# Attention's last two batches interleaved with the first expert slots, x rows scattered one iteration earlier, slot rows in grouped loads

## The reference

```python
q, k, v = heads(x, Wq, bq), heads(x, Wk, bk), heads(x, Wv, bv)      # 16 heads of 8
qp = relu(einsum('bhsd,hdf->bhsf', q, rw)) + 1e-6                   # 64 features a head
kp = relu(einsum('bhsd,hdf->bhsf', k, rw)) + 1e-6
kv = einsum('bhsf,bhsd->bhfd', kp, v)
out = einsum('bhsf,bhfd->bhsd', qp, kv) / (einsum('bhsf,bhf->bhs', qp, kp.sum(axis=2))[..., None] + 1e-6)
attention = out.reshape(b, s, 128) @ Wo + bo

probs = softmax(x @ wr + br)                                        # 8 experts
top_p, top_i = top_k(probs, 2)
gate, top1 = top_p[:, 0] / (top_p[:, 0] + top_p[:, 1]), top_i[:, 0]
for e in range(8):                                                  # w1: 128 x 512, w2: 512 x 128
    hout = gelu(x @ w1[e] + b1[e], approximate=False) @ w2[e] + b2[e]
    out = out + where(top1 == e, hout * gate, 0)
```

## Time and profile before

| | us |
|---|---|
| median of three executions | 260.04 |
| lowest, highest | 259.35, 261.4 |
| the profiled execution, its own time | 258.03 |
| its span in the profile | 256.3 |
| granted clock of PE over the span | 0.96 |
| busy: PE, PEld | 211.7 (83%), 170.2 (66%) |
| busy: DVE, ACT, POOL | 121.3 (47%), 125.4 (49%), 114.6 (45%) |
| the chain that ended last: PE, DVE, DMA | 68%, 8%, 7% |

### The profile page before, as it was taken

One profiled execution on the slowest core, in us unless ns is written; L12 is line 12 of the kernel. 1 busy time (PEld: TensorE's weight loads), 2 busy tenths in 40 slices (PEclk: granted clock), 3 DMA queues, 4 the chain that ended last, 5 costly groups with the idle time before them and its releaser, 6 DMA issues.

```text
span 256.3 us, 6785 instructions
## 1 busy us (share of the span) xinstructions
PE 211.7 (83%) x2370; PEld 170.2 (66%) x2370; DVE 121.3 (47%) x386; ACT 125.4 (49%) x291; POOL 114.6 (45%) x170
## 2 busy tenths in 40 slices
PE   0499897566899999999999689288799999999920
PEld 0365664344577676667776578187799999999920
DVE  4737532577777776777676424113233333333210
ACT  2184496333565555566655544124355555555500
POOL 3984460113667444444443425205545544445540
PEclk9999999799999999999999979769999999999995
DMA  5539999700341111111111321275888878887100
GB/s 127 157 120 345 335 278 284 207 3 12 86 146 55 64 44 42 44 44 44 43 44 64 79 72 34 63 212 145 224 259 222 234 206 236 244 237 193 57 18 0
DMA packets 27749, 34.12 MB, mean 133 GB/s; under 512 B 5523, under 2 KB 19127, under 8 KB 27718
## 3 DMA queue, kind: packets, MB, share of 16 engines
q1 hardware_dynamic: 24372, 27.24, 38.9%
q0 software_dynamic: 2944, 6.37, 7.2%
q10 hardware_dynamic: 402, 0.09, 0.2%
HBM read 22.11 MB, written 14.12 MB: 141 GB/s over the span
## 4 chain that ended last, share of the span: by engine, by line
PE 68%; DVE 8%; DMA 7%; issue 4%; ACT 4%; SPq 3%; POOL 3%; ACTq 0%; POOLq 0%; DVEq 0%
PE feat L584 12%; PE feat L480 7%; PE o_bank L598 6%; PE kv_bank L491 6%; PE kt_bank L598 6%; PE feat L469 5%; PE o_bank L515 5%; PE o_bank L524 3%; PE w_bank L533 3%; PE feat L440 2%; DVE k_feat L860 2%; DMA slot_rows<-sorted_r 2%; DMA w_slot<-w1x 2%; PE feat L441 2%; PE kt_bank L500 1%
## 5 line engine op out<-in xcount | busy, mean ns | idle before, releaser
L737 ACT ACTIVATE q_all<-feat,w_slot 128x128 f32<-128x128 f32 x156 | 44.5, 368 | 48.4 <-PE feat L584 48.4
L417 POOL DMA_INDIRECT out<-k_all,slot_rows x39 | 38.3, 983 | 47.1 <-DVE k_all L934 29.0
L584 PE MATMUL feat<-xsT,w_slot 128*128 128x128 f32 x312 | 43.4, 285 | 7.8 <-DMA w_slot<-w1x 7.8
L584 PEld LDWEIGHTS feat<-xsT,w_slot 128*128 128x128 f32 x312 | 39.6, 199 | 8.8 <-DMA w_slot<-w1x 8.3
L386 POOL DMA_INDIRECT sorted_r<-rows_all,place_i x22 | 21.9, 996 | 17.8 <-PE feat L480 13.8
L694 ACT ACTIVATE k_feat<-feat 128x1024 f32<-128x1024 f32 x16 | 16.4, 1025 | 23.5 <-PE feat L469 23.5
L701 ACT ACTIVATE q_feat<-feat 128x1024 f32<-128x1024 f32 x16 | 16.4, 1027 | 22.8 <-PE feat L480 22.8
L867 DVE TENSOR_SCALAR q_feat<-feat 128x1024 f32<-128x1024 f32 x16 | 19.6, 1225 | 14.5 <-PE feat L480 14.5
L480 PE MATMUL feat<-q_all,rw_bd 32*128 32x256 f32 x256 | 19.3, 417 | 7.6 <-DVE k_feat L860 7.6
L598 PE MATMUL o_bank<-w_sb,q_all 128*128 x160 | 22.7, 286 | 0.0
L860 DVE TENSOR_SCALAR k_feat<-feat 128x1024 f32<-128x1024 f32 x16 | 19.5, 1221 | 5.2 <-PE feat L469 5.2
(11 more groups left out here) (139 smaller groups left out, 354.1 us busy)
## 6 DMA issues: line engine op xcount, KB each, us to landing
w_slot<-w1x SPq DMA_DIRECT2D x39, 258.0 KB, 3.7
sorted_r<-ones_f SPq DMA_DIRECT2D x1, 5070.0 KB, 19.9
slot_rows<-sorted_r SPq DMA_DIRECT2D x31, 130.0 KB, 3.4
x_all<-in_x SPq DMA_DIRECT2D x8, 256.0 KB, 3.3
w1x<-in_w SPq DMA_DIRECT2D x1, 2048.0 KB, 25.7
slot_rows<-sorted_r SPq DMA_DIRECT2D x16, 65.0 KB, 2.7
out<-k_all,slot_rows POOLq DMA_INDIRECT x39, 3.2
sorted_r<-rows_all,place_i POOLq DMA_INDIRECT x22
```

The costliest lines, as they stand in the source:

```text
L417: pool.indirect_dma_start(out_rows, bass.IndirectOffsetOnAxis(ap=slot_rows[j % SLOT_RING][:, D + 1:XW].bitcast(I32), axis=0), y_sb[j % Y_R ...
L584: ins = pe.matmul(bank[:, a * P:(a + 1) * P], w1_slot[j % W1_RING][:, a * P:(a + 1) * P], xsT[j % X_RING][:, :], start=True, stop=True)
L737: act.activation(hidden_T[j % H_RING][:, a * P:(a + 1) * P], hid_bank[j % HID][:, a * P:(a + 1) * P], ACT.Gelu, bias=w1_slot[j % W1_RING][ ...
```

## The change

- **Scatters.** MERGED goes from 11 to 10 batches, so that the last scatter with an x half is that of iteration 13. The twelve tiles whose halves are scattered apart have their x half moved three each in iterations 2 and 3 and one each in 4 to 9 (a third scatter in the iteration, which waits for `kv_ps`). The r halves of batches 10 and 11 are moved in iterations 14 and 15, the last eight tiles after the loop.
- **Slot loads.** The first AHEAD slots, now 10 and not 8, lie in one tile `slots_all`. Their x halves are loaded in two DMAs (2 slots and 8 slots), their r halves in one. The rest of the ring, now 14 slots, takes the place of `v_all`.
- **SP's queue.** The weight loads for slots 4 to 9 are issued between the x loads and the wait on `r_moved`.
- **Order.** The lists of PE, ACT and DVE between the loops now interleave attention's rest with slots 0 to 4, the loop starts at j = 5, and a tiny GELU on ACT goes ahead of them. `gate_y` and `add_res` apart from each other serve 7 slots and not 4. The banks of `up`, `turn_slot` and `down` are dealt anew for the slots before 5 (TAIL), the results' ring holds 12.

```diff
-MERGED = 11
+MERGED = 10
-AHEAD = 8
-SLOT_RING = 10
-Y_RING = 8
+AHEAD = 10
+FIRST = 2
+SLOT_RING = 14
+Y_RING = 12
+TAIL = 5
-EARLY = 4
-EARLY_X = {1: range(K * MERGED, K * MERGED + 3), 2: range(K * MERGED + 3, K * MERGED + 6), 3: range(K * MERGED + 6, TILES)}
+EARLY = 7
+EARLY_X = {2: 3, 3: 3, 4: 1, 5: 1, 6: 1, 7: 1, 8: 1, 9: 1}
...
+        slots_all = sb("slots_all", [P, AHEAD, RW], F32)
+        v_flat = v_all[:, :, :].rearrange("p t n -> p (t n)")
+        slot_rows = [slots_all[:, u, :] if u < AHEAD else v_flat[:, (u - AHEAD) * RW:(u - AHEAD + 1) * RW] for u in range(SLOT_RING)]
...
-        hid_bank = [feat[0][:, 0:I], feat[0][:, I:2 * I], feat[1][:, 0:I]]
-        xsT_bank = [kv_ps_t[:, 0:P], feat[1][:, I:I + P]]
-        y_bank = [o_ps_t[:, 0:D], kt_ps_t[:, 0:D]]
+        hid_banks = [feat[0][:, 0:I], feat[0][:, I:2 * I], feat[1][:, 0:I]]
+        xsT_bank = [feat[1][:, I:I + P], kv_ps_t[:, 0:P]]
+        y_banks = [o_ps_t[:, 0:D], kt_ps_t[:, 0:D], feat[1][:, 0:D]]
...
+        def hid_bank(j):
+            return hid_banks[j % 2 if j < TAIL else (j - TAIL + 2) % HID]
+        def y_bank(j):
+            return y_banks[2 if j < TAIL - 2 else j % 2]
+        def rows_in(eng, j):
+            if j < AHEAD:
+                eng.wait_ge(x_part_in[0 if j < FIRST else 1], 16)
+            else:
+                u = j % SLOT_RING
+                eng.wait_ge(slot_in[u], 16 * (j // SLOT_RING + (0 if u < AHEAD else 1)))
...
# SP
+            def load_x_part(n):
+                js = slice(0, FIRST) if n == 0 else slice(FIRST, AHEAD)
+                sp.dma_start(slots_all[:, js, 0:XW],
+                             sorted_r[js.start * P:js.stop * P, 0:XW].rearrange("(j p) w -> p j w", p=P)).then_inc(x_part_in[n], 16)
+            def load_r_part():
+                sp.dma_start(slots_all[:, 0:AHEAD, XW:RW],
+                             sorted_r[0:AHEAD * P, XW:RW].rearrange("(j p) w -> p j w", p=P)).then_inc(r_in, 16)
...
             sp.wait_ge(x_moved, 16 * TILES)
-            for j in range(AHEAD):
-                load_x_part(j)
+            for n in range(2):
+                load_x_part(n)
+            for j in range(W1_RING, AHEAD):
+                load_w1(j)
             sp.wait_ge(r_moved, 16 * LATE * K)
-            for j in range(AHEAD):
-                load_r_part(j)
-                if j < 4:
-                    load_w1(j + W1_RING)
+            load_r_part()
+            sp.wait_ge(v_spread, NBATCH)
             for j in range(AHEAD, SLOTS):
-                load_w1(j)
                 if j == AHEAD:
                     load_slot(j)
                     load_slot(j + 1)
+                load_w1(j)
                 if j + 2 < SLOTS:
                     load_slot(j + 2)
...
# POOL
+                pace = [(kf_ps, b + 2), (qf_ps, b + 2), (kv_ps, b + 2)]
                 if 4 <= b < 4 + MERGED:
                     pool.wait_ge(r_ready, b - 3)
                     for k in range(K):
-                        pool.wait_ge((kf_ps, qf_ps)[k], b + 2)
+                        pool.wait_ge(*pace[k])
                         move_both(K * (b - 4) + k)
-            for b in range(MERGED, NBATCH):
+                for n in range(EARLY_X.get(b, 0)):
+                    pool.wait_ge(*pace[n if b < 4 else K])
+                    move_x(K * MERGED + moved[0])
+                    moved[0] += 1
+                if 4 + MERGED <= b:
+                    pool.wait_ge(r_ready, b - 3)
+                    for k in range(K):
+                        if b + 1 < NBATCH:
+                            pool.wait_ge(*pace[k])
+                        move_r(K * (b - 4) + k)
+            for b in range(NBATCH - 4, NBATCH):
...
# PE, the list between the loops after the change
+            turn_slot(0)
             outputs(14)
             pe.wait_ge(kv_ready, 2 * NBATCH)
+            turn_slot(1)
+            turn(16)
+            up(0)
             out_project(12)
             turn_outputs(14)
+            up(1)
+            turn_slot(2)
+            out_project(13)
             outputs(15)
             up(2)
             turn_slot(3)
             read_expert(0)
+            down(0)
+            turn(17)
+            turn_outputs(15)
+            up(3)
+            turn_slot(4)
+            read_expert(1)
+            down(1)
+            out_project(14)
+            turn_slot(5)
             turn(18)
+            up(4)
+            turn_slot(6)
+            read_expert(2)
+            down(2)
             out_project(15)
+            read_expert(3)
-            for j in range(3, SLOTS):
+            for j in range(5, SLOTS):
...
# ACT: after the change the list is
+            act.activation(warm[:, :], ln_eps[:, :], ACT.Gelu)
             save_outputs(14); save_turned(16); gelu(0); gelu(1); save_outputs(15); gelu(2); save_turned(17); gelu(3); save_turned(18)
# DVE: after the change the list is
             save_xsT(0); save_xsT(1); residual(12); token_rows(14); save_xsT(2); residual(13); save_xsT(3); gate_y(0)
             token_rows(15); save_xsT(4); gate_y(1); residual(14); save_xsT(5); save_xsT(6); gate_y(2); residual(15)
```

More of the change, by code:

```diff
@@ L209, in build @@
         slot_in = [sem(f"slot_in{u}") for u in range(SLOT_RING)]
-        r_in = [sem(f"r_in{u}") for u in range(AHEAD)]
+        x_part_in = [sem(f"x_part_in{n}") for n in range(2)]
+        r_in = sem("r_in")
         w1_in = [sem(f"w1_in{u}") for u in range(W1_RING)]
@@ L391, in _ @@
                 spread_v(b)
+            moved = [0]
             for b in range(NBATCH):
@@ L395, in _ @@
                     spread_v(b + 2)
[L396 removed]
+                if b == 2:
                     pool.wait_ge(placed, 2)
@@ L604, in _ @@
             pe.wait_ge(w2_in, 16)
+            pe.wait_ge(q_act, NBATCH)
+            pe.wait_ge(q_dve, NBATCH)
+            turn_slot(0)
             outputs(14)
             pe.wait_ge(kv_ready, 2 * NBATCH)
-            turn_slot(0)
+            turn_slot(1)
+            turn(16)
+            up(0)
             out_project(12)
-            pe.wait_ge(q_act, NBATCH)
-            pe.wait_ge(q_dve, NBATCH)
-            turn_slot(1)
-            up(0)
             turn_outputs(14)
-            turn(16)
+            up(1)
+            turn_slot(2)
+            out_project(13)
             outputs(15)
-            up(1)
-            out_project(13)
-            turn_slot(2)
-            turn_outputs(15)
-            turn(17)
-            out_project(14)
             up(2)
@@ L736, in gelu @@
                 for a in range(IB):
-                    act.activation(hidden_T[j % H_RING][:, a * P:(a + 1) * P], hid_bank[j % HID][:, a * P:(a + 1) * P], ACT.Gelu,
+                    act.activation(hidden_T[j % H_RING][:, a * P:(a + 1) * P], hid_bank(j)[:, a * P:(a + 1) * P], ACT.Gelu,
                                    bias=w1_slot[j % W1_RING][:, I + a:I + a + 1]).then_inc(hid_ready, 1)
+            act.activation(warm[:, :], ln_eps[:, :], ACT.Gelu)
             save_outputs(14)
+            save_turned(16)
             gelu(0)
-            save_turned(16)
+            gelu(1)
             save_outputs(15)
-            gelu(1)
+            gelu(2)
             save_turned(17)
-            gelu(2)
+            gelu(3)
             save_turned(18)
-            for j in range(3, SLOTS):
+            for j in range(4, SLOTS):
                 gelu(j)
@@ L930, in finish_y @@
                 dve.wait_ge(y_ps, j + 1)
-                if j < AHEAD:
-                    dve.wait_ge(r_in[j], 16)
                 due(dve, y_out[j % Y_RING], 16 * (j // Y_RING))
-                dve.scalar_tensor_tensor(out=y_sb[j % Y_RING], in0=y_bank[j % 2],
+                dve.scalar_tensor_tensor(out=y_sb[j % Y_RING], in0=y_bank(j),
                                          scalar=slot_rows[j % SLOT_RING][:, D:D + 1], in1=slot_rows[j % SLOT_RING][:, XW:XW + D],
@@ L938, in _ @@
             save_xsT(0)
+            save_xsT(1)
             residual(12)
-            save_xsT(1)
             token_rows(14)
+            save_xsT(2)
             residual(13)
-            save_xsT(2)
-            token_rows(15)
-            residual(14)
             save_xsT(3)
             gate_y(0)
+            token_rows(15)
             save_xsT(4)
+            gate_y(1)
+            residual(14)
+            save_xsT(5)
+            save_xsT(6)
+            gate_y(2)
             residual(15)
-            for j in range(3, SLOTS):
+            for j in range(5, SLOTS):
                 if j + 2 < SLOTS:
```

35 lines of the change are left out of this document (13 added, 22 removed).

## The result

The changed kernel takes 250.46 us in the median of four runs (249.86 to 251.57), the kernel before 259.94 beside it (259.35 to 261.4). The ratio is 0.9643 with an interval of 0.959 to 0.9695: 9.5 us gained, where 11.6 were forecast. The time of 248.4 was 2.1 us too low, inside its range.

The account below looks back on a forecast made before the run. The time was taken as set by when up(10) can start: 173.1 us against 184.68 after all terms, 11.6 gained and nothing after it, so 260.04 - 11.6 = 248.4 us; 8 in 10 range 244 to 253.6.

Parts of the forecast that it names:

- x rows early: Before the first slots: x loads start at 138.3 us instead of 144.30, ending the wait before 146.22 and the clock drop.
- Three scatters at no cost: Attention iterations with a third x scatter: POOL has room, cost taken as nothing; without that cover six times 1 us.
- The interleave, 15.1 us: PE from 143.3 us to the end of out_project(15) at 158.4: 14.2 us of work plus 0.9 for hand-over waits.
- Weight loads in time: Weight loads 4 to 9, ahead of SP's r wait, land before their up; PE's 6.2 us idle goes.
- What is late next: At turn_slot(10): slot 10's rows, behind the r load, land at 168.6 us; PE, there at 165.4, idles 3.2 us.
- rival A: Quicker r load at slot 10: 351 GB/s, a gain of 14.3 us, 245.7 us in all; chance 0.15.
- The clock, 1.4 us: After PE's idle at slot 10: 1.4 us lost to half clock, bounds 0 and 2.
- No stall in the chain of puts: After up(10): puts and the weights behind them just fit, taken as 0; 1.6 us if it fails as before.
- Rivals B: Smaller gain: the grouped load runs near 80 GB/s, gain 5.2 us, 254.8 us in all; chance 0.15.
- D: Slower than before: r load below 52 GB/s starves the queue behind it; 264.8 us at 40 GB/s; chance 0.05.
- C: x rows not early: POOL falls an iteration behind, x loads start at 144.30; gain 6.8 us, 253.2 us; chance 0.06.
- One sign that I had named against the forecast: In the profile after: the forecast is wrong if the attention iterations lengthen; no size given.

Follow-up runs that it names:

- after: The changed kernel as first timed and profiled against the kernel before: 250.46 us in the median, ratio 0.9643; its profiled execution took 251.57 us.
- Experiment 6: Changed kernel with the x rows an iteration later (MERGED back at 11, fewer third scatters), the rest kept: 264.65 us, ratio 0.9962.
- experiment 9: The changed kernel once more, unchanged, timed in more rounds on another chip: 249.97 us, ratio 0.9643.
- experiment 10: Changed kernel with the third scatter of iterations 4 to 9 issued right behind the second, not after the key product: 250.64 us, ratio 0.969.
- Experiment 11: Changed kernel with output scatters paced, slot ring 20 instead of 14 and result ring 16 instead of 12: 252.14 us, ratio 0.9763.
- experiment 12: The kernel of experiment 8 (twelve slots ahead) with the line of experiment 10 (third scatter right behind the second): 247.18 us, ratio 0.9565.
- experiment 1: The kernel before, unchanged, traced once more on another chip: 267.38 us in one run.
- experiment 5: The kernel before with only weight loads 4 to 7 moved ahead of its wait on the r scatters: 260.9 us, ratio 0.985.
- experiment 3: Changed kernel with the r load shrunk from ten slots to one, slot 0's r rows added in the others' place: 257.79 us.
- experiment 2: The changed kernel, unchanged, traced once more on another chip: 259.25 us in one run.
- experiment 7: Changed kernel with weight load 9 moved from before the r wait to behind the rows of slots 10 and 11: 259.38 us, ratio 0.9784.
- experiment 4: Changed kernel with ten r loads, one per slot, in place of the single grouped one: 262.09 us, ratio 0.9877.
- experiment 8: Changed kernel with AHEAD 12 instead of 10, slot ring 16 instead of 14 and EARLY 9 instead of 7: 257.78 us, ratio 0.9734.

## Why the prediction was right

On the chip of the result the mechanism held at each step. For the times of after I add 3.1 us, by which its `key_values(15)` is later.

- **x rows early**: forecast 138.3 + 3.1 = 141.4; measured 141.26. Experiment 6 shows their worth, 5.0 us at `up(0)`.
- **Three scatters at no cost**: true where the iterations are 5.97 us (after, 9 to 12). On chips A and B it failed: eight iterations of 6.2 us, 1.9 us in all. The named cover, room on POOL, was there; what was late was the k features' activation, 1.7 us after its product's start instead of 1.2. It is late there in the kernel before as well, in iterations 3 and 5, with 1.65 and 2.9 us (experiment 1).
- **The interleave, 15.1 us**: `up(5)` was forecast at 158.5 + 3.1 = 161.6 and its weights start at 161.28. PE is busy throughout. The 0.9 us for hand-overs covered what came.
- **Weight loads in time**: right; no wait of PE on them in after. Alone they give 4.1 us on chip B (experiment 5), since the next wait is close behind.
- **What is late next**: right in place, `turn_slot(10)`, and in its cause, the r load ahead of slot 10 (experiment 3). **The mis-sized term is slot 10's landing, 3.2 us of idle where 5.0 came.** PE arrived as forecast (168.46 against 168.5). Slot 10 came at 173.47 instead of 171.7, 1.8 us late, in two parts. The forecast's stretch was 31.0 us; all six traces of this order, or nearly this, have more, 31.8 to 33.2 (after, 2, 7, 9, 10, 11).
- **Of these, 1.0 us is the scatter.** I took 2.3 us from the last r scatter's start to SyncE's passing. In after it is 167.06 - 163.45 = 3.6, for weight loads are now on the engines at the same time (experiment 7: 2.3 again when the nearest of them is moved). This part repeats: 2.8 to 3.6 us in all traces with that load in place. `out_project(15)` was 0.3 early, which leaves 1.0.
- **The other 0.8 us is the transfer.** I counted 3.6 + 2.0 us from the issue. Measured from 167.06 it is 6.4. The single microseconds of after show how:

```profile
168.00:169.00 1.00, 0.46 (x5) 0.27 (x3) 0.00 (x0) 0.51 (x2) 0.00 (x0) 1.00 0.57 127
169.00:170.00 1.00, 0.00 (x0) 0.00 (x0) 0.00 (x0) 0.64 (x3) 0.00 (x0) 1.00 1.09 306
170.00:171.00 1.00, 0.00 (x0) 0.00 (x0) 0.00 (x0) 0.00 (x0) 0.00 (x0) 1.00 1.09 340
171.00:172.00 1.00, 0.00 (x0) 0.00 (x0) 0.00 (x0) 0.00 (x0) 0.00 (x0) 1.00 1.00 272
```

The last column is GB/s. The trace also records each packet. The first of the r load starts at 168.08, 1.0 us after the issue, and by about 171.1 the engines have together moved 798 KB: 265 GB/s in the mean, between my 223 and rival A's 351. But they did not end together. From 171 on the r load's packets still come, 40 in a microsecond where there had been 600, as from one of the 16 engines alone; its last ends at 172.66, and PE sees slot 10 at 173.47, 0.8 us later, that engine's share of slot 10 included. So the rate of 223 was too low, my fixed 2.0 us not far off (1.0 before and at most 0.8 behind), and what I had left out is that a load is in only when its slowest engine is through.

This part does not repeat: from the issue of the r load to PE's `turn_slot(10)` the six other traces with it grouped by ten have 5.2 to 5.8 us (2, 6, 7, 9, 10, 11), where I had counted 5.6. That the 5.6 was met so well is luck in part, a rate too low against a tail that I did not have.

The Trainium skill (DMA: Bandwidth & Descriptors, Anatomy of one DMA) gives 2.0 us plus bytes at 436 GB/s, and gives it for DMAs of GpSimd's path, which SyncE's loads are not. The page of the profile shows what the two grouped loads took, last column, us to landing:

```profile
slots_all<-sorted_r SPq DMA_DIRECT2D x1, 650.0 KB, 5.9
slots_all<-sorted_r SPq DMA_DIRECT2D x1, 520.0 KB, 4.0
```

For these sizes that would be 3.5 and 3.2 us, an estimate from the Trainium skill's fit; it is too short for both, and the measurement decides. By the Trainium skill too (DMA: Bandwidth & Descriptors, Queues, rings and completion order) each DMA engine takes descriptors in ring order. Experiment 3 agrees with it, since slot 10 came 1.7 us sooner once less stood ahead of it, but would agree with shared engines as well.

- **The clock, 1.4 us**: from 173.47 to `up(10)` it is 4.66 us, where the work at full speed is 3.1: 1.5 lost. I had read the clock's 0.63 between 170 and 171 as full from 170.4 on; half a clock until 170.7 gives 0.63, so the earlier trace rows held 3.0 us at half clock and a loss of 1.5 too.
- **No stall in the chain of puts**: right in after; slots 10 and 11 are 2.01 us apart, and the tail is 56.3. It was as near as the prediction said: in experiments 9 and 10 the same order waits 0.7 and 0.4 us on weights at slot 15, and the tails are 57.4 and 56.7.

The sum: 11.6 forecast, less 1.8 for slot 10 and 0.1 for the clock, is 9.7; measured 9.65. Rivals B and D did not come, and C only where it was made. What no step foresaw is the stop on two of four chips. With it and the longer iterations the ratio there is 0.978 (experiment 7, nearly the change) instead of 0.9643; that the forecast was put to a chip without them is luck. One sign that I had named against the forecast appeared, longer attention iterations: the 3.1 us in the profile of after, and the 6.2 us on chips A and B. A late start also occurs in runs of the kernel before; the even 6.2 us only with the change.

**Open** is the cause of the stop. It is in all six traces of the changed kernel and its variants on chips A and B (2, 3, 4, 6, 7, 8) and in none on the other chips. In each of them ScalarE stops 3.3 to 4.7 us after the first output scatter, and 4.0 us after it in the kernel before (experiment 1). By the work it is a different place: before slot 11's GELU with ten slots ahead, slot 14's with twelve, slot 8's in the kernel before. So it comes with POOL's unbroken scatters and neither at a fixed time nor at a fixed place in the work. ScalarE goes on within 0.15 us of the end of the run of scatters in experiments 2 to 4, but 0.8 to 2.9 us before it in 6 to 8. The short waits at runs of three or four scatters to the sorted list (experiments 1, 5 and 6) end 0.8 to 1.0 us after the last of them. Whether POOL's scatters keep signals from the other engines, or hold up something that these need then (a fetch of instructions, say), was not told apart. Within about 1 us of the beginning of all six stops lies an 8 KB packet that the trace marks as instructions, but one lies in the run of scatters of after and of experiment 9 too, where nothing stops. Experiment 11, which spreads the scatters, met a chip without the stop.

## What to carry to other kernels

When a queue stands at a wait, move what doesn't need the wait ahead of it, and then look at what is first behind it: the gain is that far and no farther (on chip B 4.1 us by order alone, 5.6 with all that lets PE last until then, and next to nothing of it is left if the x rows come an iteration later). Price a transfer by its issue to its use in the load that it will meet, not by its rate, allow for the slowest of the DMA engines, and repeat the measurement on another chip before counting on a few per cent.

## What the runs showed of the hardware

- On two of four chips ScalarE stood for 5.0 to 8.6 us and VectorE for 5.3 to 6.8 in the midst of unbroken indirect output scatters 1.29 us apart (six traces of the changed kernel and its variants), and for 3.4 in the kernel before. On the others 16, 17 and 22 such scatters in a row ran with no stop (experiments 9 and 10, after, experiment 12).
- The same kernel before took 259.44, 261.3, 264.62 and 264.95 us in the median on four chips; with the executions left out that the ratios leave out, it is 258.7, 258.4, 264.6 and 265.0.
- One load of 650 KB in place of ten saved 2.0 us of the stretch, though its pieces are the same.
- An indirect scatter's landing was seen 2.8 to 3.6 us after its start with a weight load issued beside it, and 2.3 without.
- SyncE's direct loads of 520-byte pieces reached 340 GB/s. By its packets one DMA engine ended some 1.6 us behind the others in after, and PE went on 0.8 us after that engine's last packet of the load ahead.
